# Attention's first tile: the last store of the gated MLP, its scaling, wo's splits and a k projection put elsewhere

## What is computed

```python
x = layernorm(x + mamba2_and_gated_mlp(x))        # x1 is what this line gives
x = layernorm(x + cross_attention(x, ctx, ctx))   # x2
x = layernorm(x + quantised_mlp(x))

def cross_attention(Q, K, V):                      # 16 heads of 32
    q, k, v = Q @ Wq.T + bq, K @ Wk.T + bk, V @ Wv.T + bv
    a = softmax(einsum('bqhd,bkhd->bhqk', q, k) / sqrt(32), axis=3)
    return einsum('bhqd,bdhv->bqhv', a, v) @ Wo.T + bo
```

## Time and profile before

| | us |
|---|---|
| median of 3 runs | 2724.42 (2723.39 to 2724.52) |
| the profiled execution's own time | 2722.0 |
| its span | 2720.2 |
| TensorE busy | 2659.7 (98%) |
| VectorE busy | 1523.4 (56%) |
| ScalarE busy | 1019.5 (37%) |
| GpSimd busy | 693.8 (26%) |

### The profile page before, as it was taken

The page is one execution under the profiler, slowest core; times in us unless marked ns, Lnnn a source line. Parts: engine busy times, 40 slices in busy tenths (PEclk is TensorE's granted clock), DMA queues, the critical chain, the costliest instruction groups (busy, mean ns, idle before and its releaser), DMA issues.

```text
span 2720.2 us, 42348 instructions
## 1 busy us (share of the span) xinstructions
PE 2659.7 (98%) x15264; PEld 2070.4 (76%) x15264; DVE 1523.4 (56%) x2561; ACT 1019.5 (37%) x2375; POOL 693.8 (26%) x594
## 2 busy tenths in 40 slices
PE   7999999999999999999999989999999999999999
PEld 5777777777778888888888867777777777777776
DVE  8787797797795322332233277777777774111122
ACT  6334334334434222122212255555555553222221
POOL 6553553553561101000100101322233322000000
PEclk9999999999999999999999999999999999999999
DMA  4001001101114101110111211110111124211111
GB/s 154 27 21 47 31 15 46 44 3 46 46 48 140 62 1 62 62 62 0 62 62 48 73 70 48 63 40 29 62 54 62 58 64 150 82 47 46 46 46 47
DMA packets 85482, 147.83 MB, mean 54 GB/s; under 512 B 4032, under 2 KB 17984, under 8 KB 85408
## 3 DMA queue, kind: packets, MB, share of 16 engines
q1 hardware_dynamic: 85408, 146.84, 15.7%
HBM read 113.27 MB, written 33.55 MB: 54 GB/s over the span
## 4 chain that ended last, share of the span: by engine, by line
PE 88%; DVE 8%; issue 2%; ACT 1%; DMA 1%; DVEq 0%; SPq 0%; POOL 0%; ACTq 0%; POOLq 0%
PE ps L75 22%; PE ps L77 22%; PE ps L76 22%; PE ps L1770 4%; PE ps L2133 4%; PE ps L816 2%; PE ps L1782 2%; PE ps L1761 2%; DVE mx_m L608 1%; DVE mx_cv L600 1%; PE ps L792 1%; PE ps L804 1%; PE ps L747 1%; PE ps L1714 1%; PE ps L844 1%
## 5 line engine op out<-in xcount | busy, mean ns | idle before, releaser
L1471 ACT ACTIVATE at_pr<-ps,at_nm 128x256 f32<-128x256 f32 x512 | 235.6, 473 | 201.7 <-DVE at_nm L1621 201.7
L1162 DVE TENSOR_TENSOR gm_m_lo<-gm_m,gm_m_hi 128x512 fp32r<-128x512 f32 (+1 forms) x88 | 61.1, 694 | 416.9 <-ACT gm_m_hi L1079 416.9
L75 PE MATMUL ps<-sh_u_hi,gm_gu_hi 128*128 128x512 f32 (+1 forms) x704 | 274.9, 390 | 0.0
L76 PE MATMUL ps<-sh_u_lo,gm_gu_hi 128*128 128x512 f32 (+1 forms) x704 | 274.8, 390 | 0.0
L77 PE MATMUL ps<-sh_u_hi,gm_gu_lo 128*128 128x512 f32 (+1 forms) x704 | 274.7, 390 | 0.0
L1627 DVE COPY at_pT<-ps 128x512 f32<-128x512 f32 x256 | 176.3, 689 | 138.5 <-PE ps L1770 136.4
L1073 ACT ACTIVATE gm_sg<-ps 128x512 f32<-128x512 f32 (+1 forms) x88 | 52.7, 599 | 517.6 <-PE ps L77 517.4
L543 POOL TENSOR_TENSOR mx_m<-mx_m,mx_g 128x512 f32<-128x512 f32 x128 | 185.4, 1448 | 86.3 <-DVE mx_m L610 86.1
L75 PE MATMUL ps<-sh_u_hi,qm_w_hi 128*128 128x512 f32 x512 | 201.6, 394 | 2.1 <-issue 1.1
L77 PE MATMUL ps<-sh_u_hi,qm_w_lo 128*128 128x512 f32 x512 | 199.6, 390 | 0.0
L76 PE MATMUL ps<-sh_u_lo,qm_w_hi 128*128 128x512 f32 x512 | 199.4, 389 | 0.0
(11 more groups left out here) (252 smaller groups left out, 6352.6 us busy)
## 6 DMA issues: line engine op xcount, KB each, us to landing
sh_xf<-x_scratch SPq DMA_DIRECT2D x16, 1024.0 KB, 7.5
mx_xr<-in_x SPq DMA_DIRECT2D x8, 1024.0 KB, 5.6
h_scratch<-mx_xr SPq DMA_DIRECT2D x8, 1024.0 KB, 5.1
sh_xf<-h_scratch SPq DMA_DIRECT2D x8, 1024.0 KB, 8.4
gm_xr<-in_x SPq DMA_DIRECT2D x8, 1024.0 KB, 7.3
gm_r<-h_scratch SPq DMA_DIRECT2D x8, 1024.0 KB, 6.1
x_scratch<-gm_r SPq DMA_DIRECT2D x8, 1024.0 KB, 5.2
at_cf<-in_ctxT SPq DMA_DIRECT2D x16, 512.0 KB, 3.9
```

The source lines that it names most:

```text
L75: nc.tensor.matmul(out, l_hi, r_hi, start=first, stop=False)
L76: nc.tensor.matmul(out, l_hi, r_lo, start=False, stop=False)
L1471: A(pr[h][:, t, :], SC[h][:, SEQ * t:SEQ * t + SEQ], ACT.Exp, bias=nm[:, 4 * n + h, t:t + 1], accum_out=sums[:, 2 * b + t, 4 * g + h:4 * g ...
```

## The change

- gm's last tile: SyncE does not store r there. After the pieces 4 to 7 it waits for the last low part of m (semaphore ml) and issues the loads of pieces 8 to 15.
- The store of r (now gm's function store) is issued in attention's tile 0, after the two context loads and ahead of attention's load of r. Attention's main then waits for all stores of x1 at the start of tile 1, and in tile 0 for the first seven.
- residual_norm is cut in two; in gm's last tile VectorE does the statistics alone. The scaling of row t stands in tile 0 of attention at the end of step n = t.
- wo's four pieces are rounded (ScalarE) and split (VectorE) at the ends of steps 0 to 3 of tile 0. wv1 to wk3 are still done in the prologue.
- k2's projection (slot 14, MOVED) leaves the prologue and takes tile 0's slot 5 (FREE).
- Waits: ScalarE waits for pieces 8 to 11 before the first exponentials, for wo's low parts before it writes o, and for the store of r before it writes o_hi; its waits at the start of attention are gone.

```diff
--- before.py
+++ after.py
@@ -919,7 +919,7 @@
     return me
 
 
-def residual_norm(nc, dve, s, i, r, stats, mv, rstd, out):
+def residual_statistics(nc, dve, s, i, r, stats, mv):
 
     for t in range(TT):
         dve.wait_ge(s["res"], TT * i + t + 1)
@@ -928,6 +928,11 @@
         dve.wait_ge(s["res"], TT)
         dve.wait_ge(s["bn"], TT * i + TT)
         nc.vector.bn_aggr(mv[:, t, :], stats[:, t, :]).then_inc(s["mv"], 1)
+
+
+def residual_norm(nc, dve, s, i, r, stats, mv, rstd, out):
+
+    residual_statistics(nc, dve, s, i, r, stats, mv)
     dve.wait_ge(s["rstd"], i + 1)
     for t in range(TT):
         nc.vector.tensor_scalar(out[:, t, :], r[:, t, :], mv[:, t, 0:1], rstd[:, t:t + 1], ALU.subtract,
@@ -1021,10 +1026,23 @@
 
         return TB[k % 2]
 
+    def store(sp, i):
+        sp.wait_ge(s["ln"], TT * i + TT)
+        sp.dma_start(tokens(x1)[i], r[:, :, :]).then_inc(s["st"], 16)
+
+    def norm(dve, i, t):
+
+        dve.wait_ge(s["rstd"], i + 1)
+        nc.vector.tensor_scalar(r[:, t, :], r[:, t, :], mv[:, t, 0:1], rstd[:, t:t + 1], ALU.subtract,
+                                ALU.mult).then_inc(s["ln"], 1)
+
+    me.store, me.norm = store, norm
+
     def sync(sp):
         xs, hs, os = tokens(x), tokens(h1), tokens(x1)
 
         def main(i):
+
             at(sp, s["hx"], TT * i)
             sp.dma_start(xr[:, :, :], xs[i]).then_inc(s["xr"], 16)
             at(sp, s["st"], 16 * i)
@@ -1040,8 +1058,11 @@
                 me.nxt.load_context(sp, 0, 0)
                 me.nxt.load_context(sp, 0, 1)
                 me.nxt.wt.load(sp, 8)
-            sp.wait_ge(s["ln"], TT * i + TT)
-            sp.dma_start(os[i], r[:, :, :]).then_inc(s["st"], 16)
+
+                sp.wait_ge(s["ml"], KM * NP)
+                me.nxt.wt.load(sp, 16)
+            else:
+                store(sp, i)
 
         wt.load(sp, len(pieces))
         sp.wait_ge(prev.s["st"], 16 * NP)
@@ -1189,7 +1210,10 @@
             dve.wait_ge(s["hx"], TT * i + TT)
             for t in range(TT):
                 V.tensor_tensor(r[:, t, :], ps[t][:, :], r[:, t, :], ALU.add).then_inc(s["res"], 1)
-            residual_norm(nc, dve, s, i, r, stats, mv, rstd, r)
+            if final(i):
+                residual_statistics(nc, dve, s, i, r, stats, mv)
+            else:
+                residual_norm(nc, dve, s, i, r, stats, mv, rstd, r)
 
         steps(dve, main)
 
@@ -1348,24 +1372,34 @@
     CTX = {3: (0, 1), 5: (2, 3)}
     OUT = {1: 3, 4: 0, 5: 1, 7: 2}
 
+
+
+    MOVED, FREE = 14, 5
+    FIRST = [slot for slot in range(AHEAD, SL) if slot != MOVED]
+
+    def what(i, slot):
+        return SLOT[MOVED if step_0(i) and slot == FREE else slot]
+
     def before(i, slot, more=True):
 
         if isinstance(i, int) and i < 0:
-            return slot - AHEAD
+            return before(0, FREE) if slot == MOVED else FIRST.index(slot)
         if not more:
             slot = min(slot, AHEAD)
         if isinstance(i, int) and i == 0 and slot < AHEAD:
-            return SL - AHEAD + min(slot, 5)
+            return len(FIRST) + min(slot, FREE + 1)
         return SL * i + 3 + slot
 
     def rounded(i, slot):
 
         if isinstance(i, int) and i < 0:
-            return slot - AHEAD
+            return FIRST.index(slot)
+        if step_0(i) and slot < AHEAD:
+            return len(FIRST) + (slot == FREE)
         return 8 * i + 7 + (0 if slot < AHEAD else slot - AHEAD + 1)
 
     def has(i, slot, more):
-        name = SLOT[slot][0]
+        name = what(i, slot)[0]
         return more if slot >= AHEAD else not step_0(i) if name == "o" else True
 
     def ahead(i, slot):
@@ -1373,7 +1407,7 @@
         return slot - NEXT if final(i) and slot >= NEXT else None
 
     def bank(i, slot):
-        return EARLY[(slot - AHEAD) % 4] if isinstance(i, int) and i < 0 else AB[slot % 2]
+        return EARLY[FIRST.index(slot) % 4] if isinstance(i, int) and i < 0 else AB[slot % 2]
 
     def turned(k):
         return AB[1 - k % 2]
@@ -1390,7 +1424,7 @@
     def context_high(act, i, k):
         act.wait_ge(s["cf"], 32 * i + 16 * (k // 2) + 16)
 
-        at(act, s["proj"], 0 if step_0(i) else before(i - 1, 4) + 1)
+        at(act, s["proj"], 0 if step_0(i) else before(i - 1, FREE if isinstance(i, int) and i == 1 else 4) + 1)
         nc.scalar.activation(c_hi[:, k, :], cf[:, k % 2, :], ACT.Copy).then_inc(s["chi"], 1)
 
     def context_low(pool, i, k):
@@ -1418,6 +1452,8 @@
             sp.dma_start(os[i], r[:, :, :]).then_inc(s["st"], 16)
 
         def main(i):
+
+            sp.wait_ge(prev.s["st"], 16 * NP - 16 if step_0(i) else 16 * NP)
             sp.wait_ge(s["T"], KD * (i + B) + KD)
             sp.dma_start(xf[:, :, :], os[0] if final(i) else xs[i + 1]).then_inc(s["xf"], 16)
             if not final(i):
@@ -1429,18 +1465,15 @@
                 me.nxt.load_small(sp)
                 sp.wait_ge(s["proj"], before(i, 3) + 1)
                 me.nxt.wt.load(sp, 8)
-            if not step_0(i):
+            if step_0(i):
+                prev.store(sp, NP - 1)
+            else:
                 store(i - 1)
             at(sp, s["st"], 16 * i)
             sp.dma_start(r[:, :, :], xs[i]).then_inc(s["xr"], 16)
             if final(i):
                 me.nxt.wt.load(sp, 16)
 
-        wt.load(sp, 8)
-
-        sp.wait_ge(prev.s["ml"], KM * NP)
-        wt.load(sp, len(pieces))
-        sp.wait_ge(prev.s["st"], 16 * NP)
         steps(sp, main)
 
         sp.wait_ge(s["st"], 16 * (NP - 1))
@@ -1456,7 +1489,7 @@
             A(u_hi[:, k, :], turned(k)[:, :], ACT.Copy).then_inc(s["uhi"], 1)
 
         def round_qk(i, slot):
-            name, g = SLOT[slot]
+            name, g = what(i, slot)
             if name not in ("q", "k"):
                 return
             dst, bias = (q_hi, bq) if name == "q" else (k_hi, bk)
@@ -1465,6 +1498,9 @@
 
         def exp(i, n, h):
             g, b = n // 2, n % 2
+            if step_0(i) and n == 0:
+
+                act.wait_ge(*wt.lows(8 + h))
             act.wait_ge(s["nm"], 4 * QS * i + 4 * n + h + 1)
             at(act, s["pt"], 4 * QS * i + 4 * n + h - 3)
             for t in range(2):
@@ -1479,12 +1515,18 @@
         def heads_out(i, g):
             act.wait_ge(s["pv"], QS * i + 2 * g + 2)
             at(act, s["olo"], HG * (i - 1) + g + 1)
+            if step_0(i):
+
+                act.wait_ge(*wt.lows(12 + g))
             A(o[:, g, :], O[:, :], ACT.Copy).then_inc(s["ou"], 1)
 
         def round_out(i, g):
             act.wait_ge(s["on"], HG * i + g + 1)
 
             at(act, s["proj"], 0 if step_0(i) else before(i, 8) + 1)
+            if step_0(i) and g == 0:
+
+                act.wait_ge(prev.s["st"], 16 * NP)
             A(o_hi[:, g, :], o[:, g, :], ACT.Copy).then_inc(s["ohi"], 1)
 
         def main(i):
@@ -1511,6 +1553,8 @@
                 if more and n in CTX:
                     context_high(act, i + 1, CTX[n][0])
                 exp(i, n, 3)
+                if step_0(i):
+                    wt.high(act, 13 + n)
                 if n in TURN:
                     split_u(i + 1, TURN[n][1])
                 if more and n in CTX:
@@ -1528,13 +1572,9 @@
                     me.nxt.wt.high(act, 2 * (n - 2))
 
         act.wait_ge(su.dve, dve_0 + 4)
-        for n in range(SL - AHEAD):
+        for n, slot in enumerate(FIRST):
             wt.high(act, 8 if n < 3 else 2 * n + 2)
-            round_qk(-1, AHEAD + n)
-        wt.high(act, len(pieces))
-        act.wait_ge(*wt.lows())
-
-        act.wait_ge(prev.s["st"], 16 * NP)
+            round_qk(-1, slot)
         steps(act, main)
         take_rT(NP - 1, HG - 1)
         heads_out(NP - 1, HG - 1)
@@ -1674,6 +1714,9 @@
                     halves(i, n // 2)
                 if has(i, 2 * n + 1, more):
                     take(i, 2 * n + 1)
+                if step_0(i) and n < TT:
+                    wt.low(dve, 13 + n)
+                    prev.norm(dve, NP - 1, n)
                 if not step_0(i):
                     if n == 3:
                         statistics(i - 1, 0, before(i, 5) + 1)
@@ -1688,10 +1731,9 @@
                 elif not more and n > 3:
                     me.nxt.wt.low(dve, 2 * (n - 3))
 
-        for n, slot in enumerate(range(AHEAD, SL)):
+        for n, slot in enumerate(FIRST):
             wt.low(dve, 8 if n < 3 else 2 * n + 2)
             take(-1, slot)
-        wt.low(dve, len(pieces))
         steps(dve, main)
         n = NP - 1
         take_pT(n, QS - 1, 3)
@@ -1727,8 +1769,9 @@
                 else:
                     pe.wait_ge(s["pout"], before(i, slot) - 1)
                     if step_0(i) and slot in (0, 4):
-                        pe.wait_ge(*wt.lows(10 if slot == 0 else 15))
+                        pe.wait_ge(*wt.lows(10 if slot == 0 else 11))
                 if name == "o" and g == 0:
+                    pe.wait_ge(*wt.lows(15))
                     pe.wait_ge(s["olo"], HG * i)
             if name == "q" and g == 0:
```

(4 more changed lines are left out.)

## The result

Over 21 runs of each the changed kernel takes 2719.1 us (2717.42 to 2723.18) and the kernel before 2723.31 (2721.52 to 2727.0). The ratio is 0.9986, 95% interval 0.998 to 0.9991: between 2.5 and 5.4 us faster. The forecast was 2720.4, a saving of 4.0 against the median of the runs then known (2724.42).

A forecast was written before the change was run, and what follows sets the result against it. TensorE is busy 98% of the span, so only its standstills at the border of gated MLP and attention can give time. 9.1 - 4.0 - 1.1 = 4.0 us off 2722.0 makes 2718.0, median 2.4 higher: 2720.4, range 2717.6 to 2723.4.

The forecast's parts named there:

- Step 1: Prologue between gated MLP and attention: first row maximum at 1587.1 instead of 1596.22, 9.1 us gained.
- Step 2: Attention's tile 0: the moved splits, scalings and k2 cost 4.0 us, bounds 2.4 and 7.0, leaving 5.1 gained.
- n=1 into 2: Tile 0, step 1 to step 2: later row maximum and copy hidden, copy ending 1618.84 just before values at 1618.85.
- Step 3: SyncE's queue: late store of x1 lands before ScalarE's o rounding needs it, slack 7.0 us after issue; cost nothing.
- rival C: Late store holds ScalarE at o's first block: a us per us of landing after 1643.3; chance 0.06.
- Step 4: TensorE's clock in tile 0: gaps before values in n=3 and n=4 may bring falls, 2 x 0.5 x 1.1 = 1.1 us.
- Rival A: Tile 0 pays only its lower end, 2.4 us, and the clock stays up: 6.7 us gained, 2717.7; chance 0.26.
- B: Rival: the clock falls twice in tile 0 at full price, 3.4 us: 1.7 gained, 2722.7; chance 0.10.
- D: Rival: prologue splits were not the bound, late load hidden, only k2's move counts: 1.4 us, 2723.0; chance 0.03.

The follow-up runs named there:

- loads early: Kernel before, with only the loads of pieces 8 to 15 issued ahead of gm's last store; 2719.99 us, ratio 0.9983 to the kernel before.
- scaling back: Changed kernel with the scaling of r back in gm's last tile, the store still late; 2718.74 us, ratio 0.998 to the kernel before.
- k2 back: Changed kernel with k2's projection back in the prologue and slot 5 empty again; 2720.51 us, ratio 0.9986 to the kernel before.
- scaling in gaps: Changed kernel with the four scalings moved into VectorE's waits of the prologue; 2717.26 us, ratio 0.9975 to the kernel before.
- splits later: Changed kernel, scalings in the prologue's gaps, wo2's and wo3's rounding and split moved to tile 0's steps 4 and 5; 2715.87 us, ratio 0.997.
- store behind r: Changed kernel with the store of x1 issued only after the load of r has landed; 2719.67 us, ratio 0.9987 to the kernel before.
- filler: Changed kernel with six throwaway matmuls before values in each of steps 3 and 4 of tile 0; 2717.69 us, ratio 0.9977 to the kernel before.

## Why the prediction was right

The median stands 1.3 us below the forecast of 2720.4, and 1.1 of them are the kernel before: over 21 runs its median is 2723.31, not the 2724.42 of three. The saving was forecast at 4.0 us and is 4.2 by the medians, 3.75 by the two profiles at step 5. The positions of steps 1 and 2 came out as I had walked them, the causes that I gave for them only in part; that the saving comes so near is also luck, with an interval of 2.5 to 5.4 and with the price of the clock read from one execution.

**Step 1** held. First row maximum at 17.93 behind q0, forecast 18.0 (1587.1 - 1569.09); 9.2 us gained against 9.1. Loads issued at 1565.8, no gap before k1. The one gap left is 0.75 instead of 1.15. Of the parts, loads alone bring 3.0 (loads early), the scaling's move 2.2 (scaling back, the fall taken out), k2's 2.7 (k2 back). These were made with other parts in place and need not add up; they leave 1.2 for wo's splits, which were not undone alone, and which I had put at 2.4.

**Step 2** held in its sum and in its positions, but not in what it put them down to. Tile 0 pays 3.87 us up to values of n=3 (9.20 - 5.33), forecast 4.0; at the scores of step 3 it pays 1.25, forecast 1.35, and at the row maximum of n=3 2.64, forecast 2.7. I gave the 1.35 to k2; k2 back shows 0.23 for it, and 0.93 that VectorE's additions bring without it, because by the end of step 1 they are no longer hidden. (Without the scalings k2 costs 0.73 there: the two share the same waits, and each is dear only where the other is gone.) My phrase "hidden, with nothing left over" for n=1 into 2 was right for values only; the first copy of step 2 was late, as I had noted, and I booked that lateness under k2. So the move of k2 is the better bargain (1.8 us net in the changed kernel) and the place of VectorE's four splits and scalings the worse: 1.3 for the scalings (scaling in gaps), 1.4 for two of the splits (splits later).

**Step 3** held. The store goes out at 1628.3, forecast 1636.3 - 9.1 + 0.7 = 1627.9, but for another reason: it waits for the fourth scaling. It landed 5.8 us after its issue, where I had taken 5.2. ScalarE stood 0.57 us ahead of o_hi, in front of 2.0 us of idleness; I had said it would not stand there at all. My price for rival C, a us for each us beyond the slack, was much too high: in store behind r the store lands some 4.7 us beyond it (69.8 us behind q0 against 1643.3 - 9.1 - 1569.09 = 65.1) and costs 1 us.

**Step 4** was mis-sized in its price. I took two gaps, a fall behind one in two, and 1.1 us each. The profile has one fall, behind the gap of 2.17 and not behind that of 2.28, and it cost 1.6 (7.05 - 5.47, and the same 1.59 back with the filler). 1.1 against 1.6 in this profile; over many runs it can't be read, since the profile is of one. The saving by profile is 3.75 at step 5, and the medians differ by 4.2.

The Trainium skill (TensorE: Matmul & The Clock Gate, Part 1: The HAM clock gate) has a half and a full state of the clock and says that the half one comes back after idleness. The two states agree with the traces: in all twelve the granted clock is 0.5 or 1.0 and nothing between. Which of two gaps is followed by a fall this does not tell; here the longer of the two had none. Rival A (values of n=3 moved by 6 us or more) did not come, at 5.33; B had one fall of its two; C is real and far from deciding; D is refuted by 9.2 us at the row maximum.

## What to carry to other kernels

Work moved out of a serial prologue was free here only where the receiving step had a filler on the engine that sets the pace: look per step at who waits for whom, and put small work into the waits that exist (here 2.5 us on VectorE between k0 and q3) before putting it into a loop's steps. A long wait in the chain for one load is not the worth of that load: 6.95 us waited, 3.0 gained. And where edits are worth 1 us, compare positions inside traces from a common event, not medians; how often the clock falls is read from many runs.

## What was not expected of the hardware

A gap of TensorE is followed by a fall of the clock in one execution and not in the next at the same place. The gap before k1 (1.93 and 1.94 us) had a fall behind it in scaling back and none in loads early and the kernel before. In the mixer's first tile the gap of 2.58 us had none before and one in scaling in gaps; a gap of 2.19 us there had one in the changed kernel's profile and none in filler's. Each fall lasted 3.4 us or twice that. It cost nothing where TensorE was waiting anyway (in the mixer's first tile the changed kernel is 0.93 us behind the kernel before at 55.7 us, ahead of its fall, and 0.93 at 62.7, behind it), and 1.6 us where TensorE was busy. This is a part of why equal executions differ by several us: the changed kernel's six runs with a mean granted clock of 0.997 have a median of 2722.2 us, the fifteen others 2718.9. And throwaway matmuls in a gap, as in filler, kept the clock up.

Another part arises in the first microseconds. Up to q0 TensorE has the same work in all twelve kernels, yet q0 starts between 1568.71 and 1572.35. In the five profiles in which the first eight matmuls of line 844 took 1.06 or 1.07 us it starts by 1569.09, in the seven in which they took 1.93 or 1.94 at 1569.47 or later.
